# Three more blocks of rows transposed by VectorE and DMA instead of by TensorE, in an attention-and-expert kernel

## The reference

```
x = x + xattn(ctx, layernorm(x), ...)          # q, kv, softmax, Wout
z = layernorm(x)
assign = argmax(z @ centroids.T)               # one of 8 experts per token
xhat = (z - mean) * rsqrt(var + eps)
xn   = xhat * ln_g[e] + ln_b[e]
h    = relu(xn @ w1[e].T + b1[e])              # 256 -> 1024
y    = z + h @ w2[e].T + b2[e]                 # 1024 -> 256
a    = sigmoid(z @ centroids[e])
x = x + a * y + (1 - a) * z
```

## Time and profile before

| | |
|---|---|
| median of 3 runs | 1052.74 us (1052.73 to 1053.05) |
| the profiled execution's own time | 1052.73 us |
| its span | 1050.9 us |
| PE busy | 1041.6 us, 99% |
| DVE, ACT, POOL busy | 844.9, 688.7, 565.3 us |
| 16 DMA engines, mean moved | 181 GB/s |

### The profile page before, as it was taken

The page is one execution under the profiler, slowest core; times in us unless marked ns, Lnnn a source line. Parts: engine busy times, 40 slices in busy tenths (PEclk is TensorE's granted clock), DMA queues, the critical chain, the costliest instruction groups (busy, mean ns, idle before and its releaser), DMA issues.

```text
span 1050.9 us, 24670 instructions
## 1 busy us (share of the span) xinstructions
PE 1041.6 (99%) x8610; PEld 940.5 (89%) x8610; DVE 844.9 (80%) x1979; ACT 688.7 (66%) x1838; POOL 565.3 (54%) x665
## 2 busy tenths in 40 slices
PE   9999999999999999999999999999999999999997
PEld 7889898988888888889898989889888999999997
DVE  7878888878888888888888879888887797767663
ACT  6765757675666767666757575766566666676761
POOL 1744464646454555545464646465444667566663
PEclk9999999999999999999999999999999999999999
DMA  6665657585757576767667585856356868777760
GB/s 212 160 169 148 170 156 189 146 215 142 201 146 197 142 193 155 200 156 197 159 168 185 142 210 137 213 144 171 91 153 196 307 198 294 250 234 234 249 194 31
DMA packets 159666, 190.57 MB, mean 181 GB/s; under 512 B 17454, under 2 KB 149038, under 8 KB 154673
## 3 DMA queue, kind: packets, MB, share of 16 engines
q1 hardware_dynamic: 155088, 179.09, 62.4%
q0 software_dynamic: 3360, 8.53, 2.2%
q10 hardware_dynamic: 1088, 1.31, 0.4%
HBM read 65.72 MB, written 46.07 MB: 106 GB/s over the span
## 4 chain that ended last, share of the span: by engine, by line
PE 96%; DVE 2%; POOL 1%; ACT 1%; DMA 0%; issue 0%; POOLq 0%; DVEq 0%
PE psum L742 17%; PE psum L775 16%; PE psum L812 11%; PE psum L902 10%; PE psum L791 10%; PE psum L827 9%; PE psum L761 8%; PE psum L938 6%; PE psum L932 5%; PE psum L830 1%; PE psum L883 1%; PE psum L914 1%; DVE neg_max L1410 1%; DMA c_in<-in_ctx_in 0%; PE psum L856 0%; DVE w_lo L1545 0%
## 5 line engine op out<-in xcount | busy, mean ns | idle before, releaser
L1823 POOL TENSOR_TENSOR prob<-prob,inv_sum 128x512 f32<-128x512 f32 x172 | 177.7, 1047 | 190.1 <-DVE inv_sum L1416 189.2
L1133 ACT ACTIVATE prob<-psum,neg_max 128x256 f32<-128x256 f32 x344 | 160.2, 478 | 38.8 <-DVE neg_max L1410 38.5
L1410 DVE TENSOR_REDUCE neg_max<-psum 128x2 f32<-128x512 f32 x256 | 161.9, 672 | 27.7 <-PE psum L791 27.5
L1422 DVE STREAM_TRANSPOSE prob<-prob 128x512 f32<-128x512 f32 x172 | 118.5, 698 | 12.3 <-POOL prob L1823 11.9
L1823 POOL TENSOR_TENSOR w_ring<-w_ring,inv_sum 128x512 f32<-128x512 f32 x76 | 78.1, 1041 | 76.0 <-DVE inv_sum L1416 75.7
L1140 ACT ACTIVATE head_out_hi<-psum 128x512 fp32r<-128x512 f32 x52 | 31.1, 597 | 105.6 <-PE psum L812 102.4
L1119 ACT ACTIVATE v_n<-psum 128x512 f32<-128x512 f32 x128 | 77.9, 608 | 26.7 <-PE psum L775 22.7
L1108 ACT ACTIVATE k_hi<-psum 128x512 fp32r<-128x512 f32 x128 | 77.0, 603 | 22.0 <-PE psum L742 21.3
L1461 DVE TENSOR_TENSOR k_lo<-psum,k_hi 128x512 fp32r<-128x512 f32 x128 | 85.7, 674 | 0.0
L742 PE MATMUL psum<-kv_t_hi,w_hi 128*128 128x512 f32 x252 | 85.0, 419 | 0.0
L775 PE MATMUL psum<-w_hi,kv_t_hi 128*128 128x512 f32 x256 | 80.2, 395 | 0.4 <-DVE k_lo L1461 0.4
(11 more groups left out here) (215 smaller groups left out, 2952.4 us busy)
## 6 DMA issues: line engine op xcount, KB each, us to landing
sorted_rows<-filler SPq DMA_DIRECT2D x54, 660.0 KB
prob_t<-prob SPq DMA_DIRECT2D x172, 128.0 KB, 2.8
w_ring<-prob SPq DMA_DIRECT2D x172, 128.0 KB, 2.7
w<-in_experts SPq DMA_DIRECT2D x19, 1024.0 KB, 7.8
w_ring<-in_experts SPq DMA_DIRECT2D x18, 1024.0 KB, 6.7
prob_t<-w_ring SPq DMA_DIRECT2D x76, 128.0 KB, 2.8
w_ring<-w_ring SPq DMA_DIRECT2D x76, 128.0 KB, 2.7
w_ring<-normed SPq DMA_DIRECT2D x56, 128.0 KB, 3.0
```

What stands on the lines that cost most here:

```text
L1133: act.activation(prob_at(u, bb)[:, :, parity, i], scores_i, ACT.Exp, bias=neg_max[:, at, i:i + 1], accum_out=prob_sum[:, at, i:i + 1]).the ...
L1410: dve.tensor_reduce(neg_max[:, (4 * u + n) % 8, :], psum[:, n, :].rearrange("p (i j) -> p i j", i=2), AXIS_X, ALU.max, negate=True).then_i ...
L1422: dve.transpose(probs, probs).then_inc(s_quad, 1)
L1823: pool.tensor_tensor(probs, probs, inverse, ALU.mult).then_inc(s_soft, 1)
```

## The change

Blocks 3, 4 and 5 are now handled as those from 6 on: ACT writes their rows in the strided order, DVE transposes 32 x 32 blocks, SP moves them by four DMAs each. PE's `row_transposes(3)`, `(4)` and `(5)` are gone, and their turns in the bank order too. On SP, `move_rows(3)` and `move_rows(4)` stand behind `load_rows(5)` and ahead of `load_vectors(5)` and `load_weights_1(5)`; `move_rows(5)` stands behind `load_b2(4)`. Rows are loaded before vectors in this loop. On DVE, `transpose_rows(3)` follows `split_xn(2)`, `transpose_rows(4)` follows `split_xn(3)`, `transpose_rows(5)` follows `split_xn(4)` and stands ahead of `late_blocks`; that of block 6 now follows `split_xn(5)`.

```diff
+FIRST_MOVED = 3
...
-    order += [("ft", 3), ("fy", 1, 0), ("fy", 1, 1), ("rank", n_pairs - 1), ("total",), ("ft", 4),
-              ("fy", 2, 0), ("fy", 2, 1)]
-    for slot in range(3, n_slots):
-        order += [("ft", slot + 2) if slot + 2 < n_early else ("pass", slot, 0), ("fy", slot, 0), ("fy", slot, 1), ("pass", slot, 1)]
+    order += [("fy", 1, 0), ("fy", 1, 1), ("rank", n_pairs - 1), ("total",)]
+    for slot in range(2, n_slots):
+        order += [("pass", slot, 0), ("fy", slot, 0), ("fy", slot, 1), ("pass", slot, 1)]
...
                 def move_rows(s):
-                    sp.wait_ge(f_xt, s - n_early + 1)
-                    if s == n_early:
+                    sp.wait_ge(f_xt, s - FIRST_MOVED + 1)
+                    if s == FIRST_MOVED:
                         wait_made(sp, ("wout", n_batches - 1))
                     else:
-                        sp.wait_ge(f_g, s - n_early)
+                        sp.wait_ge(f_g, s - FIRST_MOVED)
...
                 for s in range(2, n_early):
+                    load_rows(s)
+                    if s == NR + 1:
+                        move_rows(FIRST_MOVED)
+                        move_rows(FIRST_MOVED + 1)
                     load_vectors(s)
-                    load_rows(s)
                     load_weights_1(s)
                     load_weights_2(s - 1)
                     load_b2(s - 1)
+                for s in range(FIRST_MOVED + 2, n_early):
+                    move_rows(s)
...
                 layer_1(2)
-                row_transposes(3)
                 layer_2_split(1)
                 ranks(n_pairs - 1)
                 totals(("total",), n_batches - 1)
                 layer_1(3)
-                row_transposes(4)
                 layer_2_split(2)
                 for s in range(3, n_early):
                     layer_1(s + 1)
-                    if s + 2 < n_early:
-                        row_transposes(s + 2)
                     layer_2_split(s)
...
                 split_xn(2)
+                transpose_rows(3)
                 new_rows(n_batches - 1)
...
                 split_xn(3)
+                transpose_rows(4)
                 finish(1)
...
                 split_xn(4)
+                transpose_rows(5)
                 late_blocks()
                 finish(2)
                 for s in range(3, n_early):
-                    if s + 2 == n_early:
-                        transpose_rows(s + 2)
                     low_weights_1(s + 2)
                     split_hidden(s + 1)
                     split_xn(s + 2)
-                    if s + 3 > n_early:
-                        transpose_rows(s + 3)
+                    transpose_rows(s + 3)
                     finish(s)
```

More of the change, by code:

```diff
@@ L37, with bank_order @@
 FIRST_SPLIT = 1
+FIRST_MOVED = 3
 W_OUT_PIECES = 4
-def bank_order(n_pairs, last_of_early, n_early, n_slots):
+def bank_order(n_pairs, last_of_early, n_slots):
     n_steps = 4 * n_pairs
@@ L129, in build @@
     assert last_of_early % 2 == 1
-    assert 5 <= n_early <= n_sure - 2
-    order = bank_order(n_pairs, last_of_early, n_early, n_slots)
+    assert FIRST_MOVED + 3 <= n_early <= n_sure - 2
+    order = bank_order(n_pairs, last_of_early, n_slots)
     number = {item: i for i, item in enumerate(order)}
@@ L446, in wait_rows_moved @@
             def wait_rows_moved(eng, s):
-                eng.wait_ge(f_xm[s % 2], 4 * 16 * ((s - n_early) // 2 + 1))
+                eng.wait_ge(f_xm[s % 2], 4 * 16 * ((s - FIRST_MOVED) // 2 + 1))
             def wait_high(eng, g, side):
@@ L1175, in normalise_rows @@
                         wait_inputs_moved(act, n_pairs - 1)
-                    elif s < n_early + 2:
+                    elif s < FIRST_MOVED + 2:
                         wait_made(act, ("ft", s - 2))
@@ L1182, in normalise_rows @@
                         src, dst = row[:, 0:d_model], xhat[:, s % 2, i, :]
-                        if s >= n_early:
+                        if s >= FIRST_MOVED:
                             src = src.rearrange("p (c k j) -> p j c k", c=KC, j=4)
@@ L1191, in row_gain_bias @@
                     item = ("ft", s)
-                    if s < n_early:
+                    if s < FIRST_MOVED:
                         wait_made(act, item)
@@ L1622, in split_xn @@
                 def split_xn(s):
-                    if s < n_early:
+                    if s < FIRST_MOVED:
                         wait_read(dve, ("ft", s))
                     else:
-                        dve.wait_ge(f_g, s - n_early + 1)
+                        dve.wait_ge(f_g, s - FIRST_MOVED + 1)
                     if s >= 3:
```

## The result

The changed kernel takes 1058.38 us (median of 9 runs, 1056.47 to 1063.47), the one before 1052.9 (9 runs, 1052.68 to 1054.95). The ratio is 1.0052, 95% interval 1.0039 to 1.0064: 5.5 us slower, between 4.1 and 6.7. The direction was forecast. The size was not: 3.1 us were forecast, and the time lies 0.2 us above the range.

A forecast was written before the change was run, and what follows sets the result against it. PE was taken to bound the kernel: stalls of 1.9 + 0.1 + 1.5 + 0.9 = 4.4 us, less 1.26 saved, add 3.1 to 1052.73, giving 1055.8 us; range 1051.8 to 1058.2.

The forecast's parts named there:

- What bounds the kernel, and what is removed: PE runs without a gap and bounds the kernel; removing its transposes of three blocks saves 0.42 us each, 1.26 us.
- The wait for the moved rows of block 3: ACT's row_gain_bias(3) waits for move_rows(3), queued behind weights; PE stalls 1.9 us before layer_1(3).
- L: Landing time of the last move of block 3, taken as 843.5 us, between bounds of 842.0 and 844.6.
- The estimate from the Trainium skill: A 64 KB move of block 3 lands 2.15 us after issue, at 841.4, giving +0.9 us, 1053.6.
- DVE's backlog, bank order, `layer_1(5)`: DVE runs up to 4.9 us late; PE stalls 1.5 us before layer_2_split(3) and 0.9 us before layer_1(5).
- Arrives undiminished: DVE idles only 0.41 us while preparing blocks 3 to 5, so an early delay reaches the stretch's end in full.
- Hidden, by 1 us only: Before layer_1(6), split_xn(6) ends near 883.7 with PE due at 884.7, so no stall there.
- Rival 3: Loads behind move_rows(4) and the table become the wait; layer_1(6) stalls 1 to 3 us more: 1057 to 1059; chance 0.10.
- The clock: Rival: PE's clock falls to 1.2 GHz in a stall, one first layer takes 5.76 us more: 1061.5; chance 0.03.
- Rival 1: Transfers of block 3's moves are hidden if L is at most 841.7: 1052.3 or 1051.5 us, not slower; chance 0.15.
- the rule for L: Each us of L moves the end by one: 842.0 gives +1.6 us, 844.6 gives +4.2.

The follow-up runs named there:

- e6: e1 with block 5 transposed by TensorE again; ratio 0.9987 to the kernel before.
- e10: e1 with block 6's first weights loaded two places earlier and block 5's second weights and bias behind the moves of block 6; ratio 0.9996 to the kernel before.
- e1: The changed kernel with the moves of block 3 issued right behind load_rows(4), ahead of the weights of blocks 4 and 3; ratio 0.9999 to the kernel before.
- e3: The changed kernel with the work banks dealt so that (fy, 3, 0) follows (fy, 1, 0); ratio 1.0044 to the kernel before.
- e4: The changed kernel with DVE transposing only 32 of 512 columns of blocks 4 and 5; ratio 1.0033 to the kernel before.
- e7: e1 with block 4 transposed three times on DVE; ratio 1.0010 to the kernel before.
- e5: e1 with the first weights of block 6 loaded two places earlier; ratio 0.9988 to the kernel before.
- e9: The changed kernel with four constant matmuls on PE in front of the wait for split_xn(3); ratio 1.0045 to the kernel before.
- e8: e1 with block 6's first weights loaded two places earlier and block 5's second weights right behind them; ratio 1.0004 to the kernel before.

## Why the prediction was wrong, step by step

- **What bounds the kernel, and what is removed:** right. PE's transposes are worth 0.42 us a block (e6, e10).
- **The wait for the moved rows of block 3:** right, with its size. L was put at 843.5; ACT was released at 844.50 in a stage that began 0.8 us late, and at 843.31 in the second trace. The pause was 1.96 and 1.67 us for 1.9. e1 shows the cause, the place in SP's order: 5.5 us later, and behind 2 MB. The moves were seen landed 6.95 us after the first one's issue. The estimate from the Trainium skill ("DMA: Bandwidth & Descriptors", its fixed cost), 841.4, is 2 us short: no run here shows that figure for a full queue. The page fits it to transfers that GpSimd issued, and SP issues these.
- **DVE's backlog, bank order, `layer_1(5)`:** right in kind, a little large: 0.81 + 0.45 and 0.29 + 0.46 us for 1.5 + 0.9. e3 shows that the bank order only moves the pause. "Arrives undiminished" was too strong, by the traces of e4 and e7. The pauses before block 6 are 3.2 and 2.4 us together for 4.4. With the slow matmuls `layer_1(5)` starts 3.8 and 3.0 us later than before, from equal starts, where 3.1 was forecast; so up to here the sum holds in one trace and is 0.7 short in the other.
- **"Hidden, by 1 us only":** the step that failed: the wait before `layer_1(6)`, put at nothing. From equal starts `layer_1(6)` was forecast 3.1 us later than before; it is 4.8 and 4.9 us later. The chain from the table over the first weights of block 6, ACT and DVE sets it (e5 and e10 shorten this chain and the pause goes), and the sum had two of its terms too small. The table was forecast for 864.5. It was ready at 866.59 in the first trace, of which 0.8 was the late start and the rest a `late_blocks` of 7.24 us instead of 5.93, held at L1550 for 3.55 us beside two POOL instructions; and at 864.86 in the second. From the table to the end of `split_xn(6)` I took 19.2 us from one trace of the kernel before. The measured lengths are 20.5 and 21.5 us after, and 20.6 in the second trace of the kernel before. In 20.5 and 20.6 it is the weights of block 6: they landed 8.0 and 7.5 us after their issue, against 6.65 in the trace I read. In 21.5 they took 6.7, and it is the `k_lo` of 2.76 us instead of 0.69. The two terms together are 2.6 and 2.7 us too small, and the margin covers 1 of them. Rival 3 (1057 to 1059, with a chance of 0.10) named this wait. Its condition, weights of block 6 that are 2 us later than worked out, was met in the first trace (2.8 us from an equal start) and not in the second (0.6), where DVE was held instead.
- **The clock:** right as a mechanism, wrong in chance and size. I called pauses of 2 us short beside one of 5.7 and gave it 0.03 and 5.76 us. It fell in both traces, for 1.6 us of slower matmuls, and the start of `layer_1(6)` does not show them (e3, e9).
- **Rival 1 and the rule for L:** they contradict each other. "Each us of L moves the end by one" gives +1.3 us at 841.7, and rival 1 gives -0.4 for the same L. e1, in which the moved rows of block 3 are no wait, gave -0.1 us, give or take 1, in the timed runs and 0.9 in the trace, and decides neither.
- **Restarts:** not in the sum. A first layer behind a pause takes 0.2 us longer at the full clock; behind the wait before `layer_1(6)` that comes on top.

What stays open: what the clock costs in the timed runs. The spans give 4.8 and 5.6 us, and the runs spread over 7 us (before: 2.3). Their mean granted clocks say something: the four of the nine runs of the changed kernel at 0.997 or less took 1057.54, 1059.28, 1060.92 and 1063.47 us (the last at 0.995), the other five 1056.47 to 1058.7. The slowest runs of e9 (1060.47 and 1060.6, at 0.997), e4 (1059.61, at 0.995), e3 (1059.84) and e1 (1057.43, both at 0.997) look the same, and none of the 76 runs of the kernel before in the experiments is below 0.998. So the longest runs seem to have had more or later falls than the traced ones. None of them has a trace, so that is argued and not shown; filling one pause (e9) did not prevent it.

## What to carry to other kernels

A small transfer that replaces engine work is priced by its place in the issuing engine's order, not by its size: behind 2 MB of weights and 5.5 us later it cost the kernel 5.5 us, and ahead of them nothing that the runs can tell (1 us). Moving a large load out of one transfer's way puts it in another's (e8), so list everything that is queued behind the place it goes to. Where the next stage's tables and loads hang on the engine that gets the new work, follow that chain as well, and take its length from more than one trace before calling a 1 us margin hidden.

## What the runs showed of the hardware

The granted clock of TensorE fell to 1.2 GHz behind pauses of 1.67, 1.96 and 1.97 us (second trace, first trace, e4) and stayed at 2.4 GHz behind pauses of 1.51 us (e1), 1.57 (second trace, before `layer_1(6)`), 1.63, 1.68 and 2.42 us (e3): the length of the pause alone does not decide. While it was down, two matmuls of 256 columns took 0.43 us from start to start instead of 0.24. Behind a pause without a fall, the 48 matmuls of `layer_1(5)` and `layer_1(6)` took 5.98 and 5.99 us, and 5.76 in the kernel before, without a pause.

DVE instructions that ran beside one on POOL were at times held: 3.55 us for one that took 0.46 in the first trace of the kernel before, 2.76 for one of 0.69 (`k_lo` in e1, e6 and the changed kernel's second trace), 3.99 for one of 2.28. Which instruction it is changes between executions of the same kernel: in the kernel before it was L1604 for 1.92 us in one trace and L1549 for 2.73 us in the other.

The same load of 1 MB, the first weights of block 6, landed 6.65 and 7.5 us after its issue in two executions of the kernel before, and 8.0 and 6.7 us in two of the changed one.
